# A one-core decoder layer: the first batch's x1 placed by half chunks, its copies on ScalarE, and a gap in the weight table's leaves

## The reference, cut to what matters

```python
def bitnet_linear(x, weight, scale_param):
    s = jnp.maximum(jnp.mean(jnp.abs(weight), axis=1), 1e-08)
    y = jnp.einsum('bsi,oi->bso', x, jnp.sign(weight / s[:, None]))
    return jnp.nan_to_num(y * (s * scale_param)[None, None, :], ...)

# x: (2, 256, 512); 32 query heads, 8 key heads of 16; ctx: (2, 512, 128)
x = _layernorm(x + self_attention(x))            # x1: q, k, v, o are bitnet_linear
x = _layernorm(x + cross_attention(x, ctx, mask))  # x2: queries are x1 itself
x = _layernorm(x + ffn(x))                       # weights from a 16-entry table per row
```

## Time and profile before

| | us |
|---|---|
| median of 3 runs | 323.45 (322.38 to 324.1) |
| the profiled execution | 322.27 |
| its span, first to last instruction | 320.5 |
| busy: TensorE, VectorE, ScalarE, GpSimd | 277.8, 237.7, 173.1, 185.7 |
| mean granted TensorE clock | 0.94 |

### The profile page before, as it was taken

How to read it: one execution, slowest core, us unless ns; L and a number is a source line. 1 busy time by engine, 2 the same in 40 slices (tenths; PEclk the granted TensorE clock), 3 DMA queues, 4 the chain that set the end, 5 groups by cost and what they waited for, 6 DMA issues and landing times.

```text
span 320.5 us, 6205 instructions
## 1 busy us (share of the span) xinstructions
PE 277.8 (87%) x2160; PEld 174.0 (54%) x2160; DVE 237.7 (74%) x644; ACT 173.1 (54%) x308; POOL 185.7 (58%) x284
## 2 busy tenths in 40 slices
PE   7989888877998863897998999999969999998980
PEld 7679544433554430254556656666637676665930
DVE  2768479899768972898699987887997763780836
ACT  2215269857764791365547687777625664376000
POOL 8000178865994594899945998888845663310000
PEclk9979969979799995799999999999987999999997
DMA  7929941679920006700000019200000000000001
GB/s 230 368 87 121 129 47 42 80 89 203 129 58 0 0 3 112 85 3 1 3 0 2 0 42 132 29 2 2 2 0 0 2 3 0 0 35 35 0 0 66
DMA packets 15456, 17.15 MB, mean 54 GB/s; under 512 B 2112, under 2 KB 11456, under 8 KB 15424
## 3 DMA queue, kind: packets, MB, share of 16 engines
q1 hardware_dynamic: 14464, 16.29, 28.4%
q10 hardware_dynamic: 960, 0.46, 0.5%
HBM read 7.05 MB, written 1.05 MB: 25 GB/s over the span
## 4 chain that ended last, share of the span: by engine, by line
PE 57%; DVE 19%; issue 8%; POOL 7%; ACT 4%; DMA 3%; SPq 0%; DVEq 0%; ACTq 0%; POOLq 0%
PE PT L1145 15%; PE PO L1161 11%; PE PA L1100 7%; PE PS L1212 4%; DVE mx L905 4%; DMA SM<-in_wq_T 3%; PE PT L1059 3%; POOL SM L586 3%; PE PA L1103 3%; PE PT L1133 2%; PE PS L1218 2%; PE PS L1230 2%; DVE stats L933 2%; ACT QA L662 2%; PE PM L1187 1%
## 5 line engine op out<-in xcount | busy, mean ns | idle before, releaser
L653 ACT ACTIVATE PTs<-PT 128x512 f32<-128x512 f32 x192 | 110.0, 597 | 54.4 <-PE PT L1145 38.3
L586 POOL TENSOR_SCALAR SM<-SM,mx 128x512 f32<-128x512 f32 x128 | 94.5, 750 | 43.5 <-DVE mx L901 42.9
L901 DVE CUSTOM_DVE_ANT_0 SM<-PA,maskq 128x512 f32<-128x512 f32 x128 | 84.8, 687 | 33.9 <-PE PA L1100 32.8
L1145 PE MATMUL PT<-ident,SM 128*128 128x128 f32 x512 | 79.2, 280 | 1.2 <-ACT PTs L653 1.0
L1145 PEld LDWEIGHTS PT<-ident,SM 128*128 128x128 f32 x512 | 60.2, 142 | 24.1 <-issue 10.5
L1100 PE MATMUL PA<-KA,QA 96*128 96x512 bf16 x128 | 50.3, 400 | 15.7 <-DVE mx L901 8.4
L1161 PE MATMUL PO<-PTs,V 128*32 128x256 f32 x768 | 53.9, 399 | 3.0 <-ACT QA L662 2.7
L905 DVE TENSOR_REDUCE mx<-PA 128x2 f32<-128x512 f32 x64 | 40.9, 682 | 13.9 <-PE PA L1103 13.4
L1161 PEld LDWEIGHTS PO<-PTs,V 128*32 128x32 f32 x768 | 21.1, 112 | 25.9 <-issue 10.1
L522 POOL CAST SM<-mx 128x8 bf16<-128x8 f32 x16 | 5.5, 346 | 45.6 <-DVE mx L905 45.5
L1103 PE MATMUL PA<-KA,QA 96*128 96x256 bf16 x128 | 26.4, 298 | 6.4 <-DVE mx L905 6.2
(11 more groups left out here) (162 smaller groups left out, 377.2 us busy)
## 6 DMA issues: line engine op xcount, KB each, us to landing
QA<-parts SPq DMA_DIRECT2D x12, 192.0 KB, 6.4
QA<-x SPq DMA_DIRECT2D x12, 128.0 KB, 4.4
KA<-SM SPq DMA_DIRECT2D x6, 256.0 KB, 12.2
xT<-in_x_T SPq DMA_DIRECT2D x1, 1024.0 KB, 7.7
SM<-in_wq_T SPq DMA_DIRECT2D x1, 1024.0 KB, 10.7
SM<-in_wo_T SPq DMA_DIRECT2D x1, 1024.0 KB, 14.5
x<-in_x_tok SPq DMA_DIRECT2D x1, 1024.0 KB, 7.0
out<-O SPq DMA_DIRECT2D x4, 256.0 KB, 2.1
```

The lines of the kernel that those rows point to most:

```text
L586: nc.gpsimd.tensor_scalar(row, row, -1.0, mx[:, u % MX_RING, n:n + 1], ALU.mult, ALU.add).then_inc(sub_done, 1)
L653: nc.scalar.activation(PTs[:, c % PT_RING, j * 512:(j + 1) * 512], PT[:, (2 * c + j) % T_RING, :], ACT.Exp, scale=-1.0 if layer(u) else 1. ...
L901: vec.tensor_tensor_reduce(SM[:, u % SM_RING, n, :], PA[:, f % A_RING, :], maskq[:, n % QT, :], 1.0, LOWEST, ALU.add, ALU.max, mx[:, u % M ...
L1145: last = nc.tensor.transpose(PT[:, n % T_RING, (i % 4) * P:(i % 4 + 1) * P], SM[:, u % SM_RING, i, k * P:(k + 1) * P], ident[:])
```

## The change

`SIDE` is indexed by half chunks, so that a side step can stand between the two halves of a chunk. The first batch's steps are packed: `third_x1` of tile 1 moves from chunk 27 to the first half of chunk 24. `project_o` becomes two pieces of four passes. `keep_x1` moves from GpSimd to ScalarE (chunks 25, 26, 49 and 50). `LAG` becomes 0 everywhere and `MORE_STEPS` gives VectorE 26 further ticks in chunks 19 to 23 where it gave 12 in chunks 20 and 22 and 4 in 26. GpSimd makes 14 leaves wholly, with slots in units 7 to 13; ScalarE fills 18, from unit 17's third chunk to unit 26; units 14 to 16 have no slot.

```diff
-SPREAD = (((0, 2), (4, 7)), ((0, 3), (7, 10)))
+SPREAD = (((0, 1, 2, 7, 8, 9, 14), (3, 4, 5, 10, 11, 12, 16)),
+          ((1, 2, 3, 15, 17, 19, 27), (7, 8, 9, 21, 23, 25, 29)))
-MORE_STEPS = ((G + 1, (0, 0, 6, 0, 6, 0, 0, 0, 4, 0)),
+MORE_STEPS = ((G + 1, (0, 5, 6, 6, 6, 3, 0, 0, 0, 0)),
...
-POOL_LEAVES = 2 * (L1 - FIRST_LEAF)
+POOL_UNITS = range(FIRST_LEAF, L1 - 2)
+POOL_LEAVES = 2 * len(POOL_UNITS)
...
-    slots = [(u, k) for u in range(FIRST_LEAF, L1) for k in (0, 1)] + [(u, k) for u in range(L1, UNITS) for k in (0, 2)[:1 + (u < L1 + 5)]]
+    slots = [(u, k) for u in POOL_UNITS for k in (0, 1)] + [(u, k) for u in range(L1 + 1, UNITS) for k in (0, 2)[u == L1 + 1:]]
...
+            for slot, what in zip(SPREAD[b][n], ("turn_o", "project_a", "project_o") + X1_PARTS + ("keep_x1",)):
+                side_at((at + slot) // 2, what, t, slot % 2)
...
-            for t in range(QT):
-                keep_x1(t)
             for u in range(L1, UNITS):
                 shift(u)
-                if u in X1_KEPT:
-                    keep_x1(X1_KEPT[u])
...
                     nc.scalar.activation(PTs[:, c % PT_RING, j * 512:(j + 1) * 512], PT[:, (2 * c + j) % T_RING, :],
                                          ACT.Exp, scale=-1.0 if layer(u) else 1.0).then_inc(exp_done, 1)
+                    if j == 0:
+                        for what, t in SIDE[2 * c]:
+                            side(what, t)
...
+                if what == "keep_x1":
+                    act.wait_ge(x1_ready, t + 1)
+                    nc.scalar.activation(x[:, t].rearrange("p (o h d) -> p o h d", o=DT, d=HD), by_dim(O[:, t]), ACT.Copy).then_inc(x1_kept, 1)
...
+                if what == "project_a":
+                    ps_claim("project_o", t, PS_USE[("project_o", t)])
+                    pe.wait_ge(wo_scaled, DT)
+                    pe.wait_ge(ps_free, PS_USE[("turn_o", t)] + 1)
+                    for i in range(DT // 2):
+                        mm(PS[:], tile[:, i, :], woT[:, i, :], start=(i == 0), stop=False)
+                    return
```

More of the change, by code:

```diff
@@ L71 @@
 L1 = B * G
-X1_KEPT = {L1 + 9: 2, L1 + 10: 3}
 ROWS_AHEAD = 2
@@ L226, in kernel_body, with side_at @@
                 ctx, ctx_T, mask, qweight, lut4, bias, out):
-    SIDE = {c: [] for c in range(first_chunk(UNITS) + 1)}
-    def side_at(c, what, t):
-        SIDE[c].append((what, t))
+    SIDE = {c: [] for c in range(2 * first_chunk(UNITS) + 2)}
+    def side_at(c, what, t, half=1):
+        SIDE[2 * c + half].append((what, t))
     for b in range(B):
         for n, t in enumerate(range(b * QT, (b + 1) * QT)):
[L236 to L240, removed]
+            at = 2 * first_chunk(G * (b + 1) + 1)
+            for slot, what in zip(SPREAD[b][n], ("turn_o", "project_a", "project_o") + X1_PARTS + ("keep_x1",)):
+                side_at((at + slot) // 2, what, t, slot % 2)
             at = first_chunk(B * G + G * (b + 1) + 1) if b < B - 1 else first_chunk(UNITS)
@@ L245, in kernel_body @@
             side_at(at + (16 + 2 * n) * late, "ffn", t)
-    SIDE[first_chunk(UNITS)].sort(key=lambda s: ("norm_x2", "turn_x2", "ffn").index(s[0]))
+    LAST = 2 * first_chunk(UNITS) + 1
+    SIDE[LAST].sort(key=lambda s: ("norm_x2", "turn_x2", "ffn").index(s[0]))
     for o in range(DT):
@@ L251, in kernel_body @@
     PACE, FILL_PACE, CLAMP_PACE = table_pace()
-    order = [s for c in sorted(SIDE) for s in SIDE[c] if s[0] != "norm_x2"]
+    order = [s for c in sorted(SIDE) for s in SIDE[c] if s[0] not in ("norm_x2", "project_a", "keep_x1")]
     PS_USE = {what: n for n, what in enumerate(order)}
@@ L705, in _ @@
                         unload(u - 1)
-                    for what, t in SIDE[first_chunk(u) + k]:
+                    for what, t in SIDE[2 * (first_chunk(u) + k) + 1]:
                         side(what, t)
@@ L710, in _ @@
             unload(UNITS - 1)
-            for what, t in SIDE[first_chunk(UNITS)]:
+            for what, t in SIDE[LAST]:
                 side(what, t)
@@ L993, in between @@
                     for what, t in SIDE[c]:
-                        while now[0] < c + (0 if c == first_chunk(UNITS) else LAG[what]):
+                        while now[0] < c // 2 + LAG[what]:
                             yield "early"
@@ L1190, in side @@
             def side(what, t):
-                if what == "norm_x2":
+                if what in ("norm_x2", "keep_x1"):
+                    return
+                tile = oT if t % 2 == 0 else x2T
+                if what == "project_a":
[4 more added lines that the diff above has]
+                        mm(PS[:], tile[:, i, :], woT[:, i, :], start=(i == 0), stop=False)
+                    return
+                if what == "project_o":
+                    for i in range(DT // 2, DT):
+                        last = mm(PS[:], tile[:, i, :], woT[:, i, :], start=False, stop=(i == DT - 1))
+                    last.then_inc(ps_full, 1)
                     return
                 n = PS_USE[(what, t)]
-                tile = oT if t % 2 == 0 else x2T
                 if what == "turn_o":
@@ L1207, in side @@
                 bank = ps_bank(what, t)
-                if what == "project_o":
-                    pe.wait_ge(wo_scaled, DT)
-                    pe.wait_ge(ps_free, PS_USE[("turn_o", t)] + 1)
-                    for i in range(DT):
-                        last = mm(PS[:], tile[:, i, :], woT[:, i, :], start=(i == 0), stop=(i == DT - 1))
-                elif what == "ffn":
+                if what == "ffn":
                     turned = ("turn_x2", t if t < NT - QT else NT - 1)
@@ L1249, in _ @@
                             scores(v, i)
+                        if j == 0:
+                            for what, t in SIDE[2 * (first_chunk(u) + k)]:
+                                side(what, t)
                     if k % 2 == 0 and k >= 2:
```

5 lines of the change are left out of this document (1 added, 4 removed).

## The result

The changed kernel takes 318.46 us (median of 4, 317.5 to 319.51) against 323.17 for the kernel before on the same chip (322.38 to 324.1): a ratio of 0.9854, 95% interval 0.9822 to 0.9887. It is faster by 4.7 us where 9.4 were forecast, and 0.5 us above the range. The profiled executions show less, 322.27 and 319.51, because the change's is the slowest of its four and the other the fastest of its own. Medians here are of all runs; the ratios leave out the few that were slow as a whole (one of e2's took 902 us) and compare with the kernel before on the same chip, so a ratio need not be the quotient of two medians. Most lines of the new program have a number 3 lower than in the rows of before (ScalarE's exponentials are L644 for L653, its rows L656 for L662).

What follows compares the result with a forecast made beforehand. Bounds: TensorE in plain units, transfers before unit 16's scores, VectorE in units 14 to 16 (GpSimd later in 16) and 25. Terms 1.4 - 7.5 - 0.7 - 2.1 - 1.2 + 0.7 = -9.4 us gave a median of 314.0 us, range 310.5 to 318.

Steps and rivals of the forecast that it cites:

- (a): Start of chunk 28, entering the cross-attention: TensorE waits for GpSimd's late splits and starts at about 119.5 us, +1.4 us.
- rival 3: Units 13 to 15: the clock falls from TensorE's idling, +2.5 us, giving 316.5 us; chance 0.12.
- (c): Units 14 and 15: VectorE still sets the pace but loses a wait; 13.15 us becomes 12.45, -0.7 us.
- (b): TensorE's hole ahead of unit 16's scores: the first six x1 transfers land at 118.9 us, before they are needed, -7.5 us.
- Rival 1: Ahead of unit 16's scores: transfers land at 121.5 us and TensorE idles 2 us, giving 316 us; chance 0.13.
- (d): Units 16 and 17: TensorE's 2.10 us wait at the start of unit 17, caused by a leaf, goes; -2.1 us.
- (e): Units 18 and 19: waits for maxima shrink as merges move away and norms start earlier, -0.7 and -0.5 us.
- (f): Units 17 to 27: four more fills and two copies on ScalarE can put exponentials off, +0.7 us.
- (g): Unit 25 and the start of 26: VectorE's sum stays the same, 0 us, between -3.5 and +2.
- Rival 2: Unit 25: the clock keeps up and 2.5 to 3.5 us go, giving 310.8 us; chance 0.13.
- Rival 6: Chunk 28: GpSimd's lateness grows, so it starts near 123 us and the total is 321 to 323 us; chance 0.03.
- Rivals 4 and 5: Units 25 to 27, merges and GpSimd collide: 315.5 us, chance 0.06; units 19 to 27, merges await leaves: 327.5 us, 0.03.

Runs made afterwards that it cites:

- e2: The change, but with the leaves where the kernel before had them (18 on GpSimd, slots in units 14 to 16): 321.74 us, ratio 0.9916.
- e3: The change with all four copies of x1 back on GpSimd where they stood before: 314.92 us, ratio 0.9735.
- e4: The change with the first batch's two copies of x1 on ScalarE in chunks 29 and 30 instead of 25 and 26: 315.89 us, ratio 0.9772.
- e8: e3 with ScalarE copying the parts of x1 before its rows instead of after them: 317.33 us, ratio 0.9794.
- e9: The change with its four ScalarE copies of x1 made without the permutation, which does not compute the layer: 315.5 us, ratio 0.9759.
- e6: e4 with ScalarE copying the parts of x1 before its rows instead of after them: 316.22 us, ratio 0.9745.
- e5: e4 with each projection in one piece of eight passes instead of two of four: 315.85 us, ratio 0.9781.
- e1: The kernel before with only the table's leaves moved (14 on GpSimd, no slot in units 14 to 16): 319.32 us, ratio 0.989.
- e10: e5 with the second batch's two copies of x1 on GpSimd behind the shifts of units 25 and 26: 314.71 us, ratio 0.9734.
- e7: The kernel before with only its four copies of x1 moved to ScalarE, in chunks 29, 30, 49 and 50: 324.18 us, ratio 1.0027.

## Why the prediction was right and wrong

The direction, the place and the end of the hole were right. The sum was too large by 6.6 us between the profiled executions (forecast -9.4, measured -2.8), and the terms account for it, from the table above and the unit starts:

- **(a), start of chunk 28: the step that failed.** Forecast 33.1 on the table's scale, measured 38.25, 5.1 later. Of that:
  - 2.2 is ScalarE's copies and what they draw after them. "The two new copies on ScalarE in units 12 and 13 hide under this wait" was wrong twice. The price was taken from the PSUM copy at 0.60, though GpSimd's own copy of the same tile at 1.07 stood beside it; it was 1.13. And ScalarE was taken to have room. It was busy 17.28 us of the 21 between 104 and 125, with exponentials on TensorE's path. e2 against e3 and e4 shows the 2.2, in either way of taking the copies out, and so does the change against e8; e9 shows that at the assumed price it would have been 0.6. Part of the 2.2 is the second fall of the clock: from the turn in unit 13's second chunk to chunk 28 it is 1.10 us in the change and in e2, 0.77 and 0.76 in e3 and e4 at full clock, so 0.3 at least.
  - 1.7 is the clock's fall at 98 us (e2 against the change). This is rival 3's mechanism, in a place that it had not named: units 9 and 10. It came in the places that it had named too, in unit 13 (the second fall) and in units 14 and 15, for which see (c).
  - 1.0 is GpSimd: its two units (split to split) took 5.02 us each and were sized right, but unit 13's split began 0.6 later than forecast and the last split took 2.0, not 1.7.
  - 0.2 or so is rounding and the tile's wait behind the split.
- **(b), the landing.** Forecast 118.9. Issues began at 116.93 instead of near 113; by before's 5.6 us from issue to scores that is 122.6, by e6's 7.2 it is 124.1. Both are ahead of 125.56, so the wrong landing cost nothing in the change. Rival 1 (transfers gate) was not what happened there; it did happen in e6, once the rest was cleared.
- **(c), units 14 and 15.** From chunk 28 to unit 16's first transpose 13.17 us, where the forecast had 12.5: 0.7 too low. The forecast counted three merges at 0.93, 2.8 us; four stand there, since the one that fell into the hole before now meets the maxima, and they take 4.2 us (1.15, 0.96, 1.18, 0.95). In e2 the same four took 3.4 (0.72, 0.98, 0.72, 0.97), and this stretch 12.1 us. The clock was low for part of it as well, 0.63 over 137 to 140 us, where e2 had it at full. The two were not told apart, but the clock is the likelier: e5's four merges took 3.3 us, and its stretch still 13.3, at a clock of 0.87.
- **(d), unit 17.** Forecast -2.1, measured -2.2 (138.75 to 169.32 before, 138.33 to 166.71 after). No wait for a leaf is left. The best step.
- **(e), units 18 and 19.** Forecast -1.2, measured +0.7: 17 to 18 takes 10.41 for 9.80, 18 to 19 9.72 for 9.63. e1 shows both halves: its leaves alone give the -0.7 of unit 18 (9.10), and nothing in unit 19. What the second batch's new places do is then +1.3, and it stands in the trace as TensorE's 1.46 us at 174.26 for VectorE's maxima, behind the layer norm's last step (L951, 1.20 us from 172.27). The wait is 1.61 us in e2 and 0.46 in e1, so it comes with the second batch's new places and not with the leaves; which of these (the order, `LAG`, the ticks) was not tried by itself.
- **(f), the fills and copies.** Forecast +0.7, measured +0.86, all between units 19 and 20. It is the two copies and not the fills: it goes in e9 and in e10, which keep the fills, and comes in e7 (9.30 for 8.42), which has the copies alone; units 21 to 24 take 8.09. The wait of 0.73 us at 192.29 is its trace, and one of the signs that the prediction had named against itself.
- **(g), unit 25.** Forecast 0, measured -1.8. Rival 2's mechanism, in part: TensorE's gap is 2.27 us for 2.44, and the clock, 0.79 over the unit before, is 0.91. Whether the clock falls here differs between executions: in e1 (a wait of 2.27 us) and e2 (2.44) it stayed at 1.00 and the unit took 11.27 and 11.02. So some 2.5 us of a profiled execution can hang on this, and the -1.8 can't be credited to the change.

The rest, 0.5, is the start: the changed run was that much later at unit 7, ahead of all of this. In all, as measured less forecast: 5.1 + 0.7 - 0.1 + 1.9 + 0.2 - 1.8 + 0.5 = 6.5 of the 6.6. Without the copies' 2.2 the change would be at about 316.3, inside the range, and e3, e4, e9 and e10, at 314.7 to 315.9, are all close to the 314.0 that was forecast. Rival 6 ("the hole only moves") was given 0.03 and named a chunk 28 near 123; in the first batch this is nearly what happened, by ScalarE and the clock more than by GpSimd. Rivals 4 and 5 did not come: no wait for a leaf after unit 16, and between 155 and 245 us a merge takes 0.87 us on average (14 of them, 12.1 us) for 0.94 before (13, 12.2 us), with more GpSimd work beside it; the five from 230 to 253 us (units 25 to 27, rival 4's place) take 0.86. So the rule on the shared port pair, which the prediction set beside its sum, did not lengthen the moved merges on average.

What stays open: how often the clock falls at 98 us, and what decides it. It cost 1.7 us in the profiled execution, and the change's four runs lie in two pairs, 317.5 and 317.7 against 319.2 and 319.5, which would fit, but so would the clock in unit 25, and their timelines were not seen. The share of VectorE's new step places (`LAG`, `MORE_STEPS`) was not measured apart from the moved products, since TensorE would wait for x1 ahead of the scores that VectorE waits for.

## What to carry to other kernels

When a wait is filled by packing work ahead of it, list every engine whose queue gets denser there, and not only the one that waits now: here the 7.1 us of idle came back as 7.0 us of lateness, much of it by an engine (ScalarE) that the profile had at 54% overall and that was 82% busy in the stretch. The share is a warning and no proof: e4 had ScalarE at 85% (15.10 of the 17.70 us from 104 us to its chunk 28) and waited for GpSimd. What named the engine was the chain of waits, and moving its work away. Price a moved instruction from the row with the same access pattern, not from the same engine's nearest shape: the same copy was 1.07 on GpSimd, and 1.13 was the right guess for ScalarE. And when an edit that looks like tidying (no leaves in units 14 to 16) touches a full stage, try it alone first: here it gave no less than the large one (3.5 and 2.7 us).

## What the runs showed of the hardware

- **A permuted read in SBUF nearly doubles a ScalarE copy.** 128x512 fp32 from SBUF to SBUF took 1.13 to 1.17 us when each element read lay 8 elements (32 bytes) from the last, and 0.62 when they were contiguous (e9), as much as a copy out of PSUM (0.60). The permuted read also comes in rows of 16 elements, and no run tells the stride from the rows. The Trainium skill (SBUF — State Buffer, in the section on the DMA port swizzle) says that reads which move to a new 16-byte line each time pay a penalty, so that fp32 may stride little for free; the trace agrees, with 0.5 us as its size here.
- **The granted clock fell after small gaps, and in one execution and not the next.** In the profiled runs of the change and of e8 it fell at 98 us after waits of 1.19 and 0.34 us, and TensorE's four passes took 3.65 us for 1.95; in e2, e3, e4, e6 and e9 the same waits stand in the same place and the clock stayed full. In unit 25 it is alike: after 2.44 us of waiting it was low before (0.79 over the unit) and at full in e2, after 2.27 low in the change (0.91) and at full in e1 up to the unit's turn.
- **When a merge on VectorE meets a GpSimd instruction, one of the two pays up to 0.5 us, as a rule the later.** In e2 the merges at 123.75 and 130.72 took 0.72 us, and the clamps beside them 1.29 and 1.19 for 0.76; in the change the same merges took 1.15 and 1.18 (125.18 and 132.40), and the clamp beside the first its 0.76. The Trainium skill (SBUF — State Buffer, section on who interferes with whom) has the one that issues later wait for the other's whole instruction. Three of these four agree; the clamp at 123.62 began 0.13 us before the merge and still was the one that took longer. It is no stray: the timelines of all runs from 80 to 260 us have ten pairs in which GpSimd began 0.06 to 0.13 us ahead, and in each GpSimd's instruction took 1.28 to 1.31 us and the merge under 0.8. In the 22 where it was 0.14 to 0.24 us ahead, the merge was the one that took longer.
- **From SyncE's first issue to usable data took longer in the denser program.** Where TensorE waited for the scores' data, it was 5.6 to 5.7 us in before, e1 and e7, and 6.8, 7.2 and 7.4 in e5, e6 and e8 (at most 6.3 in e3, 116.15 to 122.48, without a wait), with the same twelve issues, which took 7.6 us to issue in the first three and 8.6 to 8.8 in the others. What makes the difference was not tried.
